# Routing, slot clearing and scatters placed sooner in the first attention unit

## What is computed

```python
xn = _layernorm(x, axis=-1)
x = x + _L0_attn_ref(xn, ...) + _L0_ffn_ref(xn, ...)
# attention: softmax(q k^T * 8**-0.5, causal) v, then w_proj
# experts:
logits = xt @ Wg.T
topk_logits, topk_idx = jax.lax.top_k(logits, 2)
w = jax.nn.softmax(topk_logits, axis=-1)
h = gelu(xt @ W1[e] + b1[e]);  y = sum of w * (h @ W2[e] + b2[e])
```

## Time and profile before

| | |
|---|---|
| median of three runs | 727.07 us |
| the profiled execution | 728.39 us |
| its span | 726.3 us |
| mean granted clock | 0.922 |
| TensorE busy | 685.1 us (94%) |
| VectorE busy | 535.8 us (74%) |
| ACT busy | 442.5 us (61%) |
| POOL busy | 261.0 us (36%) |

### The profile page before, as it was taken

The page is one execution under the profiler, slowest core; times in us unless marked ns, Lnnn a source line. Parts: engine busy times, 40 slices in busy tenths (PEclk is TensorE's granted clock), DMA queues, the critical chain, the costliest instruction groups (busy, mean ns, idle before and its releaser), DMA issues. The chain is left out here.

```text
span 726.3 us, 14739 instructions
## 1 busy us (share of the span) xinstructions
PE 685.1 (94%) x4927; PEld 411.9 (57%) x4927; DVE 535.8 (74%) x1811; ACT 442.5 (61%) x652; POOL 261.0 (36%) x414
## 2 busy tenths in 40 slices
PE   5998999989898999999999999999999999999997
PEld 5764444444444657556665657555575656666443
DVE  5868859787885776766776777767777767766776
ACT  5232444636354768658766757756677866776655
POOL 6822226455454123332333304332311533343311
PEclk9996567979866999999999999998999999999969
DMA  6660946031632197135442553533307175530193
GB/s 162 204 129 11 218 103 197 30 96 45 172 91 72 52 314 197 39 99 159 109 128 74 163 136 90 162 90 125 103 24 222 31 211 139 161 92 19 28 256 91
DMA packets 99274, 87.95 MB, mean 121 GB/s; under 512 B 13280, under 2 KB 86688, under 8 KB 99200
## 3 DMA queue, kind: packets, MB, share of 16 engines
q1 hardware_dynamic: 94304, 76.69, 39.6%
q0 software_dynamic: 4544, 9.35, 4.0%
q10 hardware_dynamic: 352, 0.97, 0.6%
HBM read 49.79 MB, written 20.80 MB: 97 GB/s over the span
## 5 line engine op out<-in xcount | busy, mean ns | idle before, releaser
L732 ACT ACTIVATE probs<-pool 128x1024 f32<-128x1024 f32 (+1 forms) x320 | 287.1, 939 | 183.8 <-PE pool L851 169.5
L1070 DVE CUSTOM_DVE_ANT_0 junk<-pool,cst 128x256 bf16<-128x256 f32 (+3 forms) x512 | 222.1, 486 | 60.3 <-PE pool L832 50.1
L832 PE MATMUL pool<-kT,qT 32*128 32x512 f32 (+3 forms) x768 | 199.0, 428 | 12.5 <-DVE maxes L1070 5.6
L1068 DVE TENSOR_REDUCE maxes<-pool 128x1 f32<-128x512 f32 x256 | 165.6, 685 | 44.6 <-PE pool L832 39.1
L648 POOL TENSOR_SCALAR_AFFINE_SELECT probs<-probs 128x256 f32<-128x256 f32 x208 | 81.9, 408 | 314.8 <-ACT probs L732 311.4
L868 PE MATMUL ov<-probs,v 128*32 128x512 f32 (+3 forms) x1536 | 173.8, 547 | 1.3 <-ACT ot L755 0.6
L832 PEld LDWEIGHTS pool<-kT,qT 32*128 32x128 f32 x768 | 99.5, 196 | 83.6 <-DVE maxes L1068 23.6
L851 PE MATMUL pool<-qT,kT 32*128 32x512 f32 (+3 forms) x768 | 137.4, 436 | 5.9 <-ACT probs L732 2.7
L851 PEld LDWEIGHTS pool<-qT,kT 32*128 32x128 f32 x768 | 66.8, 199 | 88.6 <-ACT probs L732 42.7
L663 POOL DMA_INDIRECT ys<-ysb,back x78 | 75.6, 969 | 69.7 <-issue 37.1
L931 PE MATMUL pool<-w2all,hid 128*128 128x128 f32 x624 | 84.9, 284 | 1.8 <-DVE attn L1096 0.5
(11 more groups left out here) (123 smaller groups left out, 597.6 us busy)
## 6 DMA issues: line engine op xcount, KB each, us to landing
w1b<-w_scr SPq DMA_DIRECT2D x39, 512.0 KB
w2all<-in_L_ffn_W SPq DMA_DIRECT2D x39, 256.0 KB, 3.2
xs<-ysb SPq DMA_DIRECT2D x13, 387.0 KB, 8.5
kT<-kqh SPq DMA_DIRECT2D x32, 128.0 KB
w_scr<-w1b SPq DMA_DIRECT2D x8, 512.0 KB
qT<-kqh SPq DMA_DIRECT2D x30, 128.0 KB
xrow<-in_L_attn_x SPq DMA_DIRECT2D x7, 512.0 KB, 5.6
xsin<-xs SPq DMA_DIRECT2D x6, 516.0 KB
```

The lines of the kernel that those rows point to most:

```text
L732: nc.scalar.activation(probs[:, s % 2, h0:h0 + m, 0:cols], pair(part)[:, :, 0:cols], ACT.Exp).then_inc(sc_done, 1)
L832: last_ = nc.tensor.matmul(bank(part)[:, at:at + cols], qT[n % 3][rows, P * i:P * i + P], kT[n % 3][rows, k0:k0 + cols], start=True, stop= ...
L1068: last_ = nc.vector.reduce_max(dst, src, axis=AX.X)
L1070: last_ = nc.vector.tensor_tensor_reduce(out=junk[:, BANKS[part][0] - RING, at:at + cols], in0=src, in1=cmask[:, W - cols:W], scale=1.0, s ...
```

## The change

Four things:
- In `ORDER`, units 0 to 3: the letters x, z, G and P of unit 0 stand sooner, and the scatters are spread from unit 0 to the beginning of unit 3 (before: 1, 27, 34 and 2 in units 0 to 3; after: 18, 19, 24 and 3). The first stands behind scores (0,3), the last behind (3,1). Everything else keeps its order. Digits are written out as ones in all units, with the same sum per unit.
- VectorE masks the stages from (0,4) to (3,3) and POOL those of unit 3 from stage 4 on; before, VectorE masked units 1 to 3.
- A new semaphore, `pos_ready`, counts the writes of `posi` for k = 0 and 1; the scatters of k = 0 wait for step 9 alone, those of k = 1 for step 10. Before, the first scatter waited for step 11.
- `deal_banks` deals adjacent banks, those whose later one has been free longest.

```diff
-CLEAR_FROM, CLEAR_UNTIL = (1, 0), (4, 0)
+CLEAR_FROM, CLEAR_UNTIL = (0, 4), (3, 4)
...
-    "mzzAmmmmoooooooo1FFmmzoxmonxwAzRo3vvFrmmAFxxxwmmowzBzGw6WveAFmm3WPxAzzxvoooFxmxxA1oxovmzAFvFAzzz3mnvFmmzWWmx"
-    "o33ArvmFAwaoo4tw5mmvmWoowo",
...
+    "mxzAmxmzmmxozoxozooxozGoPoz1FFzmxmozxmozxnwxAzRxoz111zxvvFzrxmmAFwmamowBw1a11111aWveAFamm111aWAvooaoFmA1aoov"
+    "mAaFvFA1a11mnvaFmmWWamo111a111AravmFAwaoo111a1tw11a111mmavmWooawo",
...
-        mine = sorted(sorted(among, key=lambda k: ripe[k])[:width(x)])
+        mine = min((range(k, k + width(x)) for k in among if k + width(x) - 1 in among),
+                   key=lambda r: max(ripe[k] for k in r))
...
+                    if t == 0:
+                        pool.wait_ge(pos_ready, k + 1)
                     if (t, k) == (0, 0):
-                        pool.wait_ge(slots_ready, 1)
                         for i, tiles in enumerate(NORM_TILES):
...
-                    link(nc.vector.tensor_copy(posi[:, step - 9, :], pos))
+                    nc.vector.tensor_copy(posi[:, step - 9, :], pos).then_inc(pos_ready, 1)
+                    dve.wait_ge(pos_ready, step - 8)
```

More of the change, by code:

```diff
@@ L191 @@
-    "Aggghhoohhhmohhohmm5mdooFAndFtmrvFAmmovveAFddAgggoodggdmFvAFmmovFAnoovAmFvFmmdggrA1mmmvAodgooooFmv",
-    "AFofoveffmmFAoovAontFrv325veCSftAtFFAvFAvACFSCvFAvFAvAF22SvvCectcppSS2443",
+    "mxzAmxmzmmxozoxozooxozGoPoz1FFzmxmozxmozxnwxAzRxoz111zxvvFzrxmmAFwmamowBw1a11111aWveAFamm111aWAvooaoFmA1aoov"
+    "mAaFvFA1a11mnvaFmmWWamo111a111AravmFAwaoo111a1tw11a111mmavmWooawo",
+    "FmAaRoooWavooowameonAaFWvAFarqqqtammvAmaqveFFaoooAmamvAF1a1111mammtvmammFonaAvooAaWmvoFaFooAra111vFammA11a11"
+    "111aoovm",
@@ new lines @@
+    "AavoommaFR111a11oooaAFemmanvvtra111mmaF1111a11AmFaooAveam111FamoAova1oAomaFnvFta111Aoaomvr1a11mFoamAov1a11mF"
+    "maA1111avFAmmamvUD1a11111a11mmvaooo",
+    "AoaoooomanFAooa111111rmmemFvFAmmmvFAtvemmAovFoooRnoFAmmvvrt1111oLooFAAmmmFvFA111111mmvFAv",
+    "AooFoicmveAooiohhhmmohhhooonkdmFm11111rmmmvAooFvooAogvektkUdgFAtdFoovRAkmddmFogvAFmmvmFmmLdmmAnvFmmcDioAvrAi"
+    "F",
+    "hoohooohhmmhhRhhUmogggonvvemFddLooAFtAoorvAFmmmmvAooveqqo11111FAmdgndmmFqqrvFgggAommvAodiotFvAFmmdvAmovoooFg"
@@ new lines @@
+    "dFoidDmoggAvRom",
+    "hhhmgmmhhhveoUoFdAnm11111tmFmAvrmmAoFvoovemmAFdLoooFvAFddoonAvAgmmFpdrvooFvmAmidAFgoDoovAFmmi",
+    "hhghmmmhhhgggoomhRvvoeoonh11111mmFAdprFmAUmmtmvAFoovFAoodovAtFmgddetvFmgmmALggvAmdcoovnoFAddrgmFiivFoAvAoodD"
+    "oo",
+    "hggogohhhmhmmhmmFvAommonFve11111ommFUAvArdooFovvetAgmmRdLpoFFdoodommAvAmmFvAocddDFmmovFnmAmvggrgFgoooAgvFmii"
+    "pAm",
+    "hhhoohhmmmhhooRvmmhodgnmFodg11111AoooveFmdgrAmmvFAmoqvAontFvoetFUoAvFmdgooAvAFmmLdqqvAmFmmviAFoovqdddDrtgAoo"
+    "F",
@@ new lines @@
+    "hmmmvggvihhegmoohhRhtUmmF11111oondAAoorFommvAoFovFmmmveAFmddAoonvAFmvrmmtgFoAdgggoovFAmdmovAFmmdLDgiivFAmoov"
+    "v",
+    "Aooohhmmhhhemm11111gmohonhohodFFmoomAodrvAFmmdvFUmmveooAARLdtnFmmvArvooFAddFmmvAoogovmFFoditoAgviAFdmmD",
+    "hhmmmhhhhoogoggvoFgmAnvemm11111AtrFgRgooovAFmccvFmAodgpveoFmUmvAodFddmmAptnvFLommgAvrgFooAovAoooFddDmoivAmmi"
+    "vFmm",
+    "hhooogghRgvhhhommehhoAmnmmF11111dgrUmmAtFmvAFooovvAFmmedgLdFooAgtvmFonAvoodrAFmddvFAgmoovAddDFmmmgvoAFooiivv"
+    "mmme",
+    "Aggghhoohhhmohhohmm11111mdooFAndFtmrvFAmmovveAFddAgggoodggdmFvAFmmovFAnoovAmFvFmmdggrA1mmmvAodgooooFmv",
@@ L193 @@
+    "AFofoveffmmFAoovAontFrv1111111111veCSftAtFFAvFAvACFSCvFAvFAvAF1111SvvCectcppSS1111111111111",
 ]
@@ L437, in layer_kernel @@
         cnt_ready, dlt_ready, ex_ready, slots_ready = sem("cnt_ready"), sem("dlt_ready"), sem("ex_ready"), sem("slots_ready")
+        pos_ready = sem("pos_ready")
         scattered, reloaded, gathered = [sem(f"scattered{i}") for i in range(UNDER_WAY)], [sem(f"reloaded{b}") for b in range(B)], [sem(f"gathered{b}") for b in range(B)]
```

## The result

The changed kernel took 735.09 us, the median of 20 executions (727.66 to 743.64), the kernel before in the same comparison 723.63 us (20 executions, 716.13 to 731.36). The ratio is 1.0144, with a 95% interval of 1.0108 to 1.018: **slower by 10.4 us, 7.8 to 13.0**. (It leaves disturbed executions out, and so lies under the quotient of the two medians.) The forecast of 731.7 had said 4.6 us slower, so the sign holds and the size is less than half of what came.

The account below looks back on a forecast made before the run. The prediction took VectorE to bound 53 to 66 us and TensorE 73 to 104 us. Its terms, +8.9 - 3.0 - 1.3 = +4.6 us on the median of 727.07, gave 731.7 us, range 721 to 739.

Parts of the forecast that it names:

- TensorE waits for routing steps ahead of FF: Unit 0, score pair FF: it waits behind routing steps 0 to 4 and the prefix matmuls, 7.9 us later.
- A and (0,3): Unit 0, behind FF: the next score pair A comes 8.9 us later, and scores (0,3) +8.9 us, at about 82.4.
- Step 5 costs 1.8: VectorE ahead of pair A: routing step 5 takes 1.8 us before a maximum's bank frees.
- but VectorE idled 0.83 there, so +1.0: VectorE ahead of pair A: 0.83 us of idle time gets filled, so step 5 adds only 1.0 us.
- Given back 3.0: Behind scores (0,3): 2.2 us of TensorE's waits for VectorE and 0.85 of prefix matmuls go; bounds 0 and 4.
- the gain is what it waited for VectorE: 0.4 + 1.1 + 0.7: Behind scores (0,3), where TensorE bounds: removing routing steps from VectorE saves TensorE's waits for it, 2.2 us.
- Masks at 0: Units 0 and 3: swapping masks between VectorE and POOL costs 0; bound +1.7 us per subtraction meeting a mask.
- Clears hidden: SP's queue: all 13 slot clears drain by 76 to 77 us, ahead of the row DMA at 79.9; cost 0.
- Scatters, -1.3: Unit 4: scatters run from about 83 to 205 us, saving TensorE's 1.3 us wait for their rows.
- The five scatters around the subtractions for w1 4 to 6: POOL's queue: they may delay the subtractions by up to 9 us, ahead of row DMA (1,1); taken 0, bound +3.
- clock comes up: Rival, scores (0,3) to (0,9): the granted clock rises and saves 7 to 11 us, giving 721 to 725; chance 0.25.
- a row DMA comes late: Rival: clears drain too slowly or w1 6 is late, costing 3 to 6 us, giving 734 to 738; chance 0.13.

Follow-up runs that it names:

- e6: The changed kernel with the first w1 subtraction on POOL moved behind scores (0,3); ratio 1.0192 to the kernel before.
- e1: The kernel before with only unit 0's routing steps, gate and prefix matmuls at their new places; ratio 1.0111 to the kernel before.
- e10: The changed kernel with its masks dealt to VectorE and POOL as in the kernel before; ratio 1.0099 to the kernel before.
- e9: The kernel before with unit 0's routing (steps, gate, prefix matmuls) and the slot clears at their new places; ratio 1.0106 to the kernel before.
- e5: The kernel before with VectorE also masking stages 7 to 9 of unit 0, units 1 to 3 as before; ratio 1.0168 to the kernel before.
- e2: The kernel before with only the range of stages masked on VectorE moved to (0,4) up to (3,3); ratio 1.0094 to the kernel before.
- e3: The kernel before with only the slot clears at their new places; ratio 1.0054 to the kernel before.
- e4: The changed kernel with only the routing steps, gate and prefix matmuls back at their old places; ratio 1.0046 to the kernel before.
- e7: The kernel before with routing steps 0 to 2 ahead of FF, the rest at or behind its old place; ratio 1.0066 to the kernel before.
- e8: The changed kernel with unit 0's routing and slot clears both back at their old places; ratio 1.013 to the kernel before.
- e11: The kernel before with five of the last scatters put sooner, into unit 1; routing, clears and masks stay; ratio 1.0015 to the kernel before.
- e12: The changed kernel with routing, clears and masks as before, leaving scatters and their waits at the new places; ratio 1.0096 to the kernel before.

## Why the prediction was right in sign and too small

- **TensorE waits for routing steps ahead of FF: right.** Forecast 7.9 us later at FF, measured 8.03.
- **A and (0,3): 1.4 us short.** Forecast +8.9 at (0,3), measured +10.3. Two steps failed. "Step 5 costs 1.8": it ran 2.9, because one instruction of 0.17 us was held for 1.25 beside a subtraction of POOL; e6 shows it. And "but VectorE idled 0.83 there, so +1.0": nothing of the idle time was filled, in after or in e6. A was 2.1 us late by the two; 0.7 came back up to (0,3), where TensorE waited less for the row DMA (1.63 us in place of 2.43). The first could have been seen beforehand: the subtraction stands behind FF's masks on POOL's queue, and FF was given a time.
- **Given back 3.0: at least 2 too much.** (0,3) to (0,9) took 31.6 us before. In the kernels with routing early and no early masks it took 28.3 (e1), 30.3 (e10) and 33.1 (e9), on average 30.6. But these times follow the granted clock between the two marks, 0.71, 0.62 and 0.54. In e9, whose clock is the nearest to before's 0.52, nothing came back, although VectorE was busy for 13.61 us in place of 22.74. So the 1.0 of the average may be the clock's, and a give-back isn't shown. The step that failed is "the gain is what it waited for VectorE: 0.4 + 1.1 + 0.7". Of these only the 0.4 is a wait of the matmuls; the other two rows are weight loads, which overlap the matmuls. The windows that the forecast read said the same: TensorE busy for 30.08 of 31 us leaves 0.92 to be gained.

The windows from (0,3) to (0,9) of before and of e9:

```profile
73.48:105.05 31.57, 31.13 (x129) 14.81 (x129) 22.74 (x75) 14.37 (x19) 6.10 (x9) 0.52 0.88 174
```

```profile
84.04:117.12 33.08, 31.22 (x125) 13.88 (x125) 13.61 (x50) 14.24 (x18) 6.08 (x9) 0.54 0.16 64
```

- **Masks at 0: 2 to 3.6 short.** "Both ends of units are bound by TensorE, so 0" is the step that failed. What I costed was the masks' length, and the risk that a subtraction stretches them. What they cost is their wait: a mask on VectorE waits for ACT, and the maxima behind it for the mask. In the traces it is 1.6 to 1.8 us more wait in unit 0 (2.18 in after, 2.08 in e5, 2.19 in e2, against 0.6 in e10 and 0.39 in before); in the time it is 3.6 ± 1.6 by e2, which has the wait in unit 3 with it, and 2 to 3.6 by e10. VectorE's busy share said nothing on this: it was idle half of that stretch.
- **Clears hidden: right,** and with the proper reason: e3 and e4 take the cover away, and TensorE waits 3.4 and 4.2 us longer for the row DMA.
- **Scatters, -1.3: right as to the wait,** which is gone; first and last came at 88 and 214 where 83 and 205 were forecast, the pace being 2.0 us. That the old order's wait is worth more when TensorE is early (up to 8.3 us) wasn't in the sum. e10 less e9, which is the scatters with all else equal but the masks' order around them, gives -1.8 ± 3.1: in agreement, and unproven. The five scatters around the subtractions for w1 4 to 6, taken as 0 with a bound of +3, made no wait: the row DMA (1,1) is issued at 132.03 us, 9.5 later than before, as all else there.
- **The rival "clock comes up"** half happened and brought nothing. The granted clock was 0.73 from 84 to 114 us, in before 0.67 (0.50 up to 104, and 1.00 from 104 to 114, where before is already in unit 1). (0,3) to (0,9) still took 30.6 us, of which TensorE was busy 26.11 (before 31.13 of 31.57): with TensorE faster it waited for VectorE and for ACT.

The terms as measured: 10.3 at (0,3), less some 1.0 given back without the masks, plus 3.6 for the masks, less 1.3 = 11.6, against 10.4 (7.8 to 13.0) by the ratio and 9.1 at equal clock. The terms come from single profiles and from differences with errors of 2 us and more, so this says only that no large term is missing. The marks agree: at (1,9) and (3,2) after is 10.3 and 10.2 us late, and less the 1.3 of the rows that is 8.9 to 9.0. The forecast of 4.6 lay under the interval. Its range held the result, by way of a rival ("a row DMA comes late", 734 to 738) whose mechanism did not occur.

What stays open: the 1 to 2.5 us between that sum and the time, whether anything is given back at equal clock, and what decides the clock that an execution is granted. An order that beats before wasn't found.

## What to carry to other kernels

An instruction that waits for another engine is costed by who stands behind it in its queue, and not by its own length or by how idle its engine is: a mask of 0.4 us that waits for ACT delayed the maxima that gave TensorE its banks. When several pieces are moved at once, ask for each what hides it now: here clears were hidden by late rows, and rows were late by the routing. A chain that keeps its pace ends sooner only if it starts sooner: five scatters placed sooner in its middle moved its end by 1.8 us, from 230.33 to 228.57. And before a wait is counted as a gain, look at which row it stands in, the matmul's or the weight load's, and at how much of the stretch the engine isn't busy.

## What the runs showed of the hardware that was not expected

- One VectorE instruction on 128x8 elements took 1.25 us beside a two-input POOL operation of 1.26 us, in four profiles (after, e1, e9, e10), and 0.17 us without it (before, e6).
- In the fourteen profiles, fourteen masks on VectorE (128x256, 0.42 us undisturbed) overlapped such a POOL operation by more than 0.1 us. Each ended 0.29 us after it, whatever had been left to do. Eleven of them had started 0.3 to 0.75 us ahead of the operation's recorded start, while a scatter was being issued, and still took 1.89 to 3.53 us. The 451 masks that met a scatter's issue alone took 0.41 to 0.50 us.
- A row DMA issued behind three clears of 387 KB each (and ten before them) landed so that its reader waited 5.8 and 6.7 us, where it was 2.4 to 3.2 with the clears at their old places and the row DMA at its old time (before, e2, e5, e7, e8, e11, e12). This fits the ring order of the Trainium skill ("DMA: Bandwidth & Descriptors", section on queues, rings and completion order) that the forecast cited and no row of before could show. That the transfers only shared the bandwidth isn't ruled out.
- Over the 202 executions, 0.01 more of the mean granted clock goes with 4.4 us less time (3.1 over the 160 that the ratios use), over a span of 726 us. Over 20 executions of one kernel the mean clock ran from 0.908 to 0.934 and the time from 743.64 to 727.66 us.
